# Windowed attention: how the reciprocals of the softmax sums reach the context's layout

## The chip, the core and the metric

The kernel runs on one core of a Trainium2 chip. The metric is the device time of one execution in microseconds, the median of three runs. A core has five engines that run side by side and meet at semaphores: TensorE (PE, matrix products and transposes into PSUM), VectorE (DVE), ScalarE (ACT), GpSimd (POOL) and SyncE (SP), which here only issues DMAs.

## What is computed

A chain of small layers over x of 8 sequences of 256 tokens with 128 features: a plain attention and a mixture of experts, a linear attention, a windowed transformer, a rotary attention, a second windowed transformer, a latent attention, and a last plain attention with experts. The change is in the two windowed transformers. Each has 6 layers; a layer has 16 heads of 64 and looks back over windows of 32 keys. Its attention, cut to what matters (dots mark what is left out):

```python
sim = jnp.einsum('bhwie,bhwje->bhwij', bq, bk2) * QK_SCALE
sim = jnp.where(mask, -jnp.finfo(sim.dtype).max, sim)
attn = jax.nn.softmax(sim, -1)
out = jnp.einsum('bhwij,bhwje->bhwie', attn, bv2)
...
return out @ Wo
```

The division by the sum of each softmax row is what the change is about: the kernel multiplies the context by the reciprocals afterwards.

## The kernel before

`windowed_transformers` goes through 48 **turns** per transformer, one for each layer and sequence (`TURNS = DEPTH * B`, turn T is layer T // 8, sequence T % 8). A turn has 8 **slots**, one for each pair of heads p. Every engine has its own hand-written order of work: `pe_window`, `act_window`, `dve_window` and the loop over `pool_spread` and `pool_prepare` go through the slots of turn T. In its slots they also prepare the queries, keys and values of turn T + 1 (`pe_chunks` L1784, the squares, copies and rotations at L2003, L2007, L2121, L2129, the turned queries and keys L1807, L2015, L2115) and do the output projection and feed-forward part of the turns before (`pe_out` L1819, `pe_gates` L1850, and others). An engine that waits holds back all that stands behind it in its order.

One pair goes this way. The 128 partitions hold the queries of one half (t = 0 or 1) of the 256 tokens.

- PE makes the scores (L1716); DVE adds the mask and takes the row minimum (L2090); ACT makes the exponentials and their row sums (`act_probs` L1983), into `pair_sums`, four columns per pair: two halves by two heads ("sides").
- DVE takes the four reciprocals in slot p (`dve_recip` L2099). They stand with queries on the partitions.
- PE turns the exponentials (L1728, L1729) in slot p, ACT copies them out of PSUM (L1990), and in slot p + 1 PE weighs the values with them (`pe_weigh` L1750). The context stands in PSUM bank 4 or 5, columns 0 to 255, with the 64 features of the two heads on the partitions and the 256 queries along the row.
- So the reciprocals have to be turned too, and repeated over 64 partitions. POOL spreads them to 128 x 256 (`pool_spread` L1944), PE transposes the two halves into the other half of the same bank (`pe_shares` L1738, slot p + 1), ACT copies them to `shares` (`act_copy_shares` L1995, at the end of slot p + 1), and DVE multiplies (`dve_share` L2104, slot p + 2, directly behind the reciprocal of that slot).

SP issues only the weights' loads, each as soon as its tile is free; they come at the start of each layer, so once in 8 turns, and are all in one sequence.

Of the kernel before, what the change touches and what calls it, by code (L numbers as in the profile page):

```python
# [16 lines left out]
P = 128  # L17
# [6 lines left out]
DH = 64  # L24
# [69 lines left out]
def allocate(nc, ctx):  # L94
# [36 lines left out]
    c.pair_sums = sb("pair_sums", [P, 4, HALVES, 2])  # L131
    c.shares = sb("shares", [P, 2, S])
    c.recip = sb("recip", [P, 2, 32])
    c.spread = sb("spread", [P, 2, S])
# [1475 lines left out]
WEIGHT_ORDER = (2, 0, 4, 3, 1, 5)  # L1610
PE_CHUNK_SLOTS = {j: (2 * j, 2 * j + 1) for j in range(6)}
# [15 lines left out]
def windowed_transformers(nc, sem, c, name, io):  # L1627
# [7 lines left out]
             "probs_ready", "probsT_in_psum", "probsT_ready", "prev_ready", "recip_ready", "spread_ready", "ctx_in_psum", "shares_ready", "ctx_ready",  # L1635
# [8 lines left out]
     s.probs_ready, s.probsT_in_psum, s.probsT_ready, s.prev_ready, s.recip_ready, s.spread_ready, s.ctx_in_psum, s.shares_ready, s.ctx_ready,  # L1644
     s.out_in_psum, s.shifted_in_psum, s.normed, s.normedT_in_psum, s.normedT_ready,
     s.gates_in_psum, s.linear_in_psum, s.gelu_ready, s.hidden_ready, s.ff_out_in_psum) = [sem(name + "_" + n) for n in names]
    wqkv_loaded = [sem(name + "_wqkv_loaded" + str(k)) for k in range(CHUNKS)]
    step = Count(steps)
    wqkv, wo = c.wA[:, :], c.wB[:, :]
    w1, w2 = c.wC[:, :], c.wD[:, :]  # L1650

# [44 lines left out]
    def run(number):  # L1696
        T0, T1 = number * TURNS, (number + 1) * TURNS

        def has_turn(turn):
            return T0 <= turn < T1  # L1700
# [31 lines left out]
        def pe_shares(pe, T, p):  # L1732
            pe.wait_ge(s.spread_ready, T * PAIRS + p + 1)
            if T * PAIRS + p - 1 > T0 * PAIRS:

                pe.wait_ge(s.ctx_ready, T * PAIRS + p - 1)
# [150 lines left out]
        def pe_window(pe, T):  # L1887
            following = has_turn(T + 1)
            for p in range(PAIRS):
                pe_turn_probs(pe, T, p)  # L1890
                if p >= 1:
                    pe_shares(pe, T, p - 1)
                elif has_turn(T - 1):
                    pe_shares(pe, T - 1, PAIRS - 1)
# [27 lines left out]
        def pe_tail(pe):  # L1922
            L = T1 - 1
            pe_shares(pe, L, PAIRS - 1)
# [13 lines left out]

        def pool_spread(g, T, p):
            g.wait_ge(s.recip_ready, T * PAIRS + p + 1)  # L1940
            if T * PAIRS + p - 2 >= T0 * PAIRS:

                g.wait_ge(s.ctx_in_psum, T * PAIRS + p - 1)
            g.tensor_copy(c.spread[:, p % 2, :].rearrange("p (n d) -> p n d", n=4),  # L1944
                          c.recip[:, 0, 4 * (p % 4):4 * (p % 4) + 4].unsqueeze(2).broadcast_to((P, 4, DH))
                          ).then_inc(s.spread_ready, 1)
# [31 lines left out]
        def act_probs(a, T, p, side):  # L1978
            if side == 0:
                a.wait_ge(s.negmax_ready, T * PAIRS + p + 1)  # L1980
            for t in range(HALVES):
                tile = c.pairs[:, 2 * (p % 4) + side, AT[t]:AT[t] + SPAN[t]]
                last = a.activation(tile, tile, ACT.Exp, scale=-1.0, bias=c.negmax[:, 2 * p + side, t:t + 1],  # L1983
                                    accum_out=c.pair_sums[:, p % 4, t, side:side + 1])
# [55 lines left out]
        def act_window(a, T):  # L2040
            following = has_turn(T + 1)
            for p in range(PAIRS):
# [19 lines left out]
                if p >= 1:  # L2062
                    act_copy_shares(a, T, p - 1)
                elif has_turn(T - 1):
                    act_copy_shares(a, T - 1, PAIRS - 1)
# [6 lines left out]
        def act_tail(a):  # L2072
            L = T1 - 1
            act_copy_shares(a, L, PAIRS - 1)
# [22 lines left out]
        def dve_recip(v, T, p):  # L2097
            v.wait_ge(s.probs_ready, T * PAIRS + p + 1)
            v.reciprocal(c.recip[:, 0, 4 * (p % 4):4 * (p % 4) + 4],  # L2099
                         c.pair_sums[:, p % 4, :, :].rearrange("p t h -> p (t h)")).then_inc(s.recip_ready, 1)  # L2100

        def dve_share(v, T, p):
            v.wait_ge(s.shares_ready, T * PAIRS + p + 1)
# [163 lines left out]

        with nc.Block() as block:

            @block.sync  # L2270
            def _(sp):
                sp.dma_start(c.rope[:, :, :, 0:DH], w["rope"]).then_inc(tables_loaded, 16)
                for d in range(layer_of(T0), layer_of(T1)):
                    T, first = d * B, d * B == T0

                    if not first:
                        sp.wait_ge(s.tables_ready, d)
                    sp.dma_start(c.scl[:, :, :].rearrange("p a b -> p (a b)"),
                                 w["scales"][d].partition_broadcast(P)).then_inc(s.scales_loaded, 16)
                    for k in WEIGHT_ORDER:  # L2280

                        if not first:
                            sp.wait_ge(s.chunk_in_psum, (T - 1) * N_CHUNKS + CHUNK_ORDER.index((1, k)) + 1)
                        sp.dma_start(wqkv[:, k * 512:(k + 1) * 512],
                                     w["wqkv"][d][:, k * 512:(k + 1) * 512]).then_inc(wqkv_loaded[k], 16)

                    if not first:
                        sp.wait_ge(s.out_in_psum, T)
                    sp.dma_start(wo, w["wo"][d]).then_inc(s.wo_loaded, 16)

                    if not first:
                        sp.wait_ge(s.linear_in_psum, T)
                    sp.dma_start(w1, w["w1"][d]).then_inc(s.ff_loaded, 16)

                    if not first:
                        sp.wait_ge(s.hidden_ready, T * 3)
# [228 lines left out]
```

## Time and profile before

| | us |
|---|---|
| median of 3 runs | 6057.9 (6055.31 to 6059.08) |
| the profiled execution's span | 6062.1 |
| PE, DVE, ACT, POOL busy in it | 5372.5, 4241.2, 3913.4, 2700.1 |
| head pairs in the two windowed transformers | 768 |

All durations come from one profiled execution with the span above. Matmuls are pipelined: the rows of successive ones overlap, and what one costs is the distance between their starts. A row with "x2" merges two instructions that follow each other. What stands in brackets is the idle time of the engine ahead of the row, and what ended it.

### The profile page before, as it was taken

How to read it: one execution, taken by the hardware profiler on the slowest of the kernel's cores; microseconds unless marked ns; L12 is line 12 of the kernel's file. 1: busy time of each engine (PE TensorE's matmuls, PEld its weight loads, DVE VectorE, ACT ScalarE, POOL GpSimd, SP SyncE). 2: the span in 40 equal slices, each digit the busy share in tenths (PEclk: the TensorE clock that was granted, in tenths of full speed). 3: DMA queues.
4: the chain of work that ended last, by engine and by line, in shares of the span. 5: the costliest groups of instructions: out<-in, count | busy, mean ns of one | idle time of the engine just before them, and what ended most of it. 6: DMA issues, size and time to landing. Idle time of an engine off the chain costs nothing. (4 is left out here: it accounts for less than half of the span.)

```text
span 6062.1 us, 121575 instructions
## 1 busy us (share of the span) xinstructions
PE 5372.5 (89%) x41154; PEld 3794.5 (63%) x41154; DVE 4241.2 (70%) x16112; ACT 3913.4 (65%) x11510; POOL 2700.1 (45%) x2578
## 2 busy tenths in 40 slices
PE   7885699999999999997489999999999999697989
PEld 5674366666666666665256666666666666464678
DVE  4453688888888888885378888788888887454522
ACT  2211588888888888884178888888888888222333
POOL 0000556556565565652166656566565665230000
PEclk9996799999999999998599999999999999697999
DMA  0000000000000000000000000000000000000000
GB/s 11 22 1 3 22 1 12 9 12 9 1 15 6 12 9 12 8 1 4 21 1 7 10 6 12 9 12 9 4 13 6 12 8 1 5 2 4 2 29 8
DMA packets 30964, 53.45 MB, mean 9 GB/s; under 512 B 7688, under 2 KB 17168, under 8 KB 29712
## 3 DMA queue, kind: packets, MB, share of 16 engines
q1 hardware_dynamic: 30352, 45.66, 2.4%
q8 instruction: 339, 5.55, 0.4%
q14 instruction: 273, 2.24, 0.1%
HBM read 44.60 MB, written 1.05 MB: 8 GB/s over the span
## 5 line engine op out<-in xcount | busy, mean ns | idle before, releaser
L1784 PE MATMUL bank<-wA,next_rowT 128*128 128x512 f32 x2304 | 1213.7, 629 | 194.6 <-DVE turnB L2129 73.1
L1983 ACT ACTIVATE pairs<-pairs,negmax 128x128 f32<-128x128 f32 (+1 forms) x3072 | 1236.8, 418 | 18.6 <-DVE negmax L2090 17.5
L1960 POOL TENSOR_TENSOR turnA<-raw,ropes 128x512 f32<-128x512 f32 x768 | 968.7, 1271 | 169.3 <-ACT raw L2007 140.4
L2090 DVE CUSTOM_DVE_ANT_0 pairs<-bank,bands,big 128x128 f32<-128x128 f32 (+1 forms) x3072 | 941.7, 364 | 64.6 <-PE bank L1716 61.0
L1967 POOL TENSOR_TENSOR qk<-turnA,turnB 128x512 f32<-128x512 f32 x768 | 975.8, 1271 | 0.0
L1944 POOL COPY spread<-recip 128x256 f32<-128x256 f32 x768 | 305.3, 398 | 1257.8 <-DVE recip L2099 1251.4
L1784 PEld LDWEIGHTS bank<-wA,next_rowT 128*128 128x128 f32 x2304 | 369.6, 190 | 676.7 <-DVE turnB L2129 294.3
L1990 ACT ACTIVATE pairsT<-bank 128x512 f32<-128x512 f32 x768 | 465.9, 607 | 302.2 <-PE bank L1729 301.9
L1983 ACT ACTIVATION_READ_ACCUMULATOR pairs<-pairs,negmax 128x1 f32 x3072 | 625.0, 203 | 0.0
L285 POOL TENSOR_TENSOR rstd<-vareps,neg_half 128x2 f32<-128x2 f32 x56 | 39.0, 696 | 1292.4 <-DVE vareps L256 892.7
L2129 DVE TENSOR_TENSOR turnB<-bank,ropes 128x512 f32<-128x512 f32 x768 | 523.1, 681 | 0.0
L1973 POOL TENSOR_TENSOR qk<-qk,big 128x1024 f32<-128x1024 f32 x192 | 365.7, 1905 | 341.3 <-DVE recip L2204 327.9
L1807 PE MATMUL bank<-ident,qk 128*128 128x128 f32 x3072 | 431.1, 279 | 41.5 <-ACT big L2010 16.4
L2007 ACT ACTIVATE raw<-bank 128x512 f32<-128x512 f32 x768 | 461.1, 600 | 0.0
L1807 PEld LDWEIGHTS bank<-ident,qk 128*128 128x128 f32 x3072 | 344.7, 142 | 156.1 <-issue 131.6
L1728 PE MATMUL bank<-ident,pairs 128*128 128x128 f32 x1536 | 383.4, 277 | 27.7 <-ACT pairs L1983 27.7
L1729 PE MATMUL bank<-ident,pairs 128*128 128x128 f32 x1536 | 377.7, 273 | 0.0
L1819 PEld LDWEIGHTS bank<-wB,ctxT 128*128 128x128 f32 x3072 | 357.8, 192 | 8.4 <-issue 0.3
L1819 PE MATMUL bank<-wB,ctxT 128*128 128x128 f32 x3072 | 358.8, 275 | 0.0
L1728 PEld LDWEIGHTS bank<-ident,pairs 128*128 128x128 f32 x1536 | 216.1, 141 | 178.3 <-ACT pairs L1983 90.8
L2104 DVE TENSOR_TENSOR ctxT<-bank,shares 128x256 f32<-128x256 f32 x768 | 306.1, 399 | 8.6
L1850 PE MATMUL bank<-xT,wC 128*128 128x256 f32 (+1 forms) x1152 | 305.4, 402 | 6.9 <-ACT big L2038 3.7
(306 smaller groups left out, 11272.8 us busy)
## 6 DMA issues: line engine op xcount, KB each, us to landing
wA<-in_wt_wqkv SPq DMA_DIRECT2D x72, 256.0 KB, 2.8
wB<-in_wt_wo SPq DMA_DIRECT2D x12, 512.0 KB, 3.5
wC<-in_wt_w SPq DMA_DIRECT2D x12, 341.0 KB, 2.9
wD<-in_wt_w SPq DMA_DIRECT2D x12, 192.0 KB, 2.4
big<-in_e_up SPq DMA_DIRECT2D x1, 2048.0 KB
big<-in_e_down SPq DMA_DIRECT2D x1, 2048.0 KB
scl<-in_wt_scales SPq DMA_DIRECT2D x12, 128.0 KB, 3.1
X<-in_x SPq DMA_DIRECT2D x8, 128.0 KB, 2.5
```

Of the source, the lines that this page charges most:

```text
L1728: pe.transpose(out[:, 0:P], probs[:, 0:P], c.ident[:, :])
L1729: last = pe.transpose(out[:, P:2 * P], probs[:, P + WINDOW:2 * P + WINDOW], c.ident[:, :])
L1784: pe.matmul(side_bank(i)[:, :], c.next_rowT[:, t * P:(t + 1) * P], wqkv[:, k * 512:(k + 1) * 512], start=True, stop=True).then_inc(s.chunk ...
L1807: done = pe.transpose(side_bank(i)[:, (2 * k + t) * P:(2 * k + t + 1) * P], c.qk[:, t, which, at:at + P], c.ident[:, :])
L1819: done = pe.matmul(c.bank[6][:, t * D:(t + 1) * D], ctxT[T % 2][:, k, t * P:(t + 1) * P], wo[:, k * D:(k + 1) * D], start=(k == 0), stop=( ...
L1960: g.tensor_tensor(c.turnA[:, m % 2, :].rearrange("p (h d) -> p h d", h=8), c.raw[:, m % 4, :].rearrange("p (h d) -> p h d", h=8), cos, ALU ...
L1967: g.tensor_tensor(c.qk[:, t, k // 2, (k % 2) * 512:(k % 2) * 512 + 512], c.turnA[:, m % 2, :], c.turnB[:, m % 4, :], ALU.add).then_inc(s.s ...
L1983: last = a.activation(tile, tile, ACT.Exp, scale=-1.0, bias=c.negmax[:, 2 * p + side, t:t + 1], accum_out=c.pair_sums[:, p % 4, t, side:si ...
L1990: a.activation(whole_blocks(c.pairsT[:, 2 * (p % 2):2 * (p % 2) + 2, :]), c.bank[2][:, :].rearrange("p (n k) -> p n k", n=4), ACT.Identity ...
L2007: last = a.activation(c.raw[:, m % 4, :], src, ACT.Identity)
L2090: last = v.tensor_tensor_reduce(c.pairs[:, 2 * (p % 4) + side, AT[t]:AT[t] + SPAN[t]], c.bank[side][:, AT[t]:AT[t] + SPAN[t]], c.bands[:, ...
L2129: v.tensor_tensor(out, turned, sin.unsqueeze(1).broadcast_to((P, 8, 2, DH // 2)), ALU.mult).then_inc(s.chunk_rotated, 1)
```

## The change

The spread copy, the two transposes and the copy of the shares are taken out, with their semaphores and the tile `spread`. In their place SP stores the four reciprocals of a pair, [128, 4], to a row of a small ring in DRAM so that each column becomes a line of 128 numbers (512 runs of 4 bytes), waits for it to land, and loads two lines that follow each other, 256 numbers, into each half of `shares`, repeated over 64 partitions. `pair_sums` changes the order of its columns to suit. `dve_share` waits for the context in PSUM and for the two loads. PE's wait for a free bank moves from `pe_shares` to `pe_weigh`. SP's program now goes slot by slot (`sp_window`): store, then the weights' loads that fall into this slot, then the two loads.

```diff
-        def pe_shares(pe, T, p):
-            pe.wait_ge(s.spread_ready, T * PAIRS + p + 1)
...
-            for t in range(HALVES):
-                pe.transpose(c.bank[4 + p % 2][:, S + t * P:S + (t + 1) * P], c.spread[:, p % 2, t * P:(t + 1) * P],
-                             c.ident[:, :])
         def pe_weigh(pe, T, p):
             pe.wait_ge(s.probsT_ready, T * PAIRS + p + 1)
             pe.wait_ge(s.prev_ready, T * PAIRS + p + 1)
+            if T * PAIRS + p - 1 > T0 * PAIRS:
+
+                pe.wait_ge(s.ctx_ready, T * PAIRS + p - 1)
...
-        def pool_spread(g, T, p):
...
-        def act_copy_shares(a, T, p):
-            a.wait_ge(s.ctx_in_psum, T * PAIRS + p + 1)
-            a.activation(c.shares[:, p % 2, :], c.bank[4 + p % 2][:, S:2 * S], ACT.Identity).then_inc(s.shares_ready, 1)
...
         def dve_share(v, T, p):
-            v.wait_ge(s.shares_ready, T * PAIRS + p + 1)
+            v.wait_ge(s.ctx_in_psum, T * PAIRS + p + 1)
+            v.wait_ge(s.shares_loaded[p % 2], 32 * (T * (PAIRS // 2) + p // 2 + 1))
             v.tensor_tensor(ctxT[T % 2][:, p, :], c.bank[4 + p % 2][:, 0:S], c.shares[:, p % 2, :],
                             ALU.mult).then_inc(s.ctx_ready, 1)
...
+        def sp_store_recip(sp, T, p):
+
+            sp.wait_ge(s.recip_ready, T * PAIRS + p + 1)
+            with nc.allow_non_contiguous_dma(reason="one column of reciprocals becomes one line"):
+                sp.dma_start(ring[p % 4].rearrange("n q -> q n"),
+                             c.recip[:, 0, 4 * (p % 4):4 * (p % 4) + 4]).then_inc(s.recip_stored, 16)
+
+        def sp_load_shares(sp, T, p):
+
+            sp.wait_ge(s.recip_stored, 16 * (T * PAIRS + p + 1))
+            if T * PAIRS + p - 1 > T0 * PAIRS:
+
+                sp.wait_ge(s.ctx_ready, T * PAIRS + p - 1)
+            for side in range(2):
+                sp.dma_start(c.shares[DH * side:DH * side + DH, p % 2, :],
+                             ring[p % 4, 2 * side:2 * side + 2, :].rearrange("t q -> (t q)").partition_broadcast(DH)
+                             ).then_inc(s.shares_loaded[p % 2], 16)
...
+        def sp_window(sp, T):
+            def layer_starts(turn):
+                return T0 < turn < T1 and starts_layer(turn)
+            for p in range(PAIRS):
+                sp_store_recip(sp, T, p)
+                if layer_starts(T + 2):
+                    if p == 0:
+                        sp_scales(sp, T + 2, False)
+                    for k in SP_WQKV_SLOTS.get(p, ()):
+                        sp_wqkv(sp, T + 2, k, False)
+                if layer_starts(T) and p == 7:
+                    sp_wo(sp, T, False)
+                if layer_starts(T - 2):
+                    if p == 0:
+                        sp_w1(sp, T - 2, False)
+                    if p == 1:
+                        sp_cols(sp, T - 2, False)
+                    if p == 3:
+                        sp_w2(sp, T - 2, False)
+                sp_load_shares(sp, T, p)
```

## Rows read from the trace of the kernel before

**Rows 1.** Page, section 1: engine, busy us, share of span, instructions.
```profile
span 6062.1 us, 121575 instructions
PE 5372.5 (89%) x41154; PEld 3794.5 (63%) x41154; DVE 4241.2 (70%) x16112; ACT 3913.4 (65%) x11510; POOL 2700.1 (45%) x2578
```

**Rows 2.** Windows: stretch, length, busy us per engine, clock, DMA share, GB/s.
```profile
1617.10:1642.10 25.00, 23.56 (x161) 14.89 (x160) 24.07 (x88) 22.06 (x71) 20.01 (x20) 1.00 0.00 1
1642.10:1652.50 10.40, 10.06 (x79) 8.46 (x79) 6.00 (x34) 6.85 (x18) 5.91 (x5) 1.00 0.01 2
```

**Rows 3.** Timeline of PE, slots 6 and 0: start us, us, instruction, idle before.
```profile
1644.83 0.27 PE L1729 MATMUL bank<-ident,pairs 128*128 128x128 f32 x1
1644.94 0.38 PE L1738 MATMUL bank<-ident,spread 128*128 128x128 f32 x2
...
1646.62 1.99 PE L1850 MATMUL bank<-xT,wC 128*128 128x256 f32 x8
...
1656.32 0.33 PE L1728 MATMUL bank<-ident,pairs 128*128 128x128 f32 x1 [0.21 <-ACT pairs L1983]
```

**Rows 4.** Timeline of ACT, slots 6, 7 and 0.
```profile
1645.63 0.56 ACT L2029 ACTIVATE xT<-bank,cols 128x256 f32<-128x256 f32 x1
...
1656.08 0.19 ACT L1983 ACTIVATION_READ_ACCUMULATOR pairs<-pairs,negmax 128x1 f32 x1
...
1661.61 0.36 ACT L1995 ACTIVATE shares<-bank 128x256 f32<-128x256 f32 x1
1661.87 0.58 ACT L2003 ACTIVATE sq<-bank 128x512 f32<-128x512 f32 x1
```

**Rows 5.** Timeline of DVE: reciprocals and multiplications of one turn.
```profile
1612.90 0.17 DVE L2099 RECIPROCAL recip<-pair_sums 128x4 f32<-128x4 f32 x1
...
1617.10 0.18 DVE L2099 RECIPROCAL recip<-pair_sums 128x4 f32<-128x4 f32 x1 [1.08 <-ACT pairs L1983]
1617.37 0.42 DVE L2104 TENSOR_TENSOR ctxT<-bank,shares 128x256 f32<-128x256 f32 x1
...
1622.05 0.40 DVE L2104 TENSOR_TENSOR ctxT<-bank,shares 128x256 f32<-128x256 f32 x1
...
1631.10 0.17 DVE L2099 RECIPROCAL recip<-pair_sums 128x4 f32<-128x4 f32 x1
1631.19 0.39 DVE L2104 TENSOR_TENSOR ctxT<-bank,shares 128x256 f32<-128x256 f32 x1
...
1633.64 0.18 DVE L2099 RECIPROCAL recip<-pair_sums 128x4 f32<-128x4 f32 x1
...
1638.69 0.40 DVE L2104 TENSOR_TENSOR ctxT<-bank,shares 128x256 f32<-128x256 f32 x1
```

**Rows 6.** Page, section 5: busy us, mean ns of one, idle before.
```profile
L1944 POOL COPY spread<-recip 128x256 f32<-128x256 f32 x768 | 305.3, 398 | 1257.8 <-DVE recip L2099 1251.4
```

**Rows 7.** DMA issues: KB each, median us from issue to landing.
```profile
wA<-in_wt_wqkv SPq DMA_DIRECT2D x72, 256.0 KB, 2.8
...
scl<-in_wt_scales SPq DMA_DIRECT2D x12, 128.0 KB, 3.1
...
out<-X SPq DMA_DIRECT2D x8, 128.0 KB, 2.0
...
rope<-in_window_rope SPq DMA_DIRECT2D x2, 256.0 KB, 3.1
...
cols<-in_wt_cols SPq DMA_DIRECT2D x12, 4.0 KB, 1.6
...
rows<-in_a_bo SPq DMA_DIRECT2D x2, 64.0 KB, 3.6
```

**Rows 8.** Timeline of SP: the second column is the issue.
```profile
1130.53 0.43 SPq L2278 DMA_DIRECT2D scl<-in_wt_scales  x1
```

**Rows 9.** Timeline of DVE, end of the first transformer.
```profile
2803.11 0.17 DVE L2099 RECIPROCAL recip<-pair_sums 128x4 f32<-128x4 f32 x1
...
2805.92 0.92 DVE L2104 TENSOR_TENSOR ctxT<-bank,shares 128x256 f32<-128x256 f32 x2
```

More of the change, by code:

```diff
@@ L1610 @@
 WEIGHT_ORDER = (2, 0, 4, 3, 1, 5)
+SP_WQKV_SLOTS = {2: (2, 0), 3: (4,), 5: (3, 1), 6: (5,)}
 PE_CHUNK_SLOTS = {j: (2 * j, 2 * j + 1) for j in range(6)}
@@ L1647, in windowed_transformers @@
     wqkv_loaded = [sem(name + "_wqkv_loaded" + str(k)) for k in range(CHUNKS)]
+    s.shares_loaded = [sem(name + "_shares_loaded" + str(n)) for n in range(2)]
     step = Count(steps)
@@ new lines, in sp_scales, with sp_wqkv @@
+        def sp_scales(sp, T, first):
+            if not first:
+                sp.wait_ge(s.tables_ready, layer_of(T))
+            sp.dma_start(c.scl[:, :, :].rearrange("p a b -> p (a b)"),
+                         w["scales"][layer_of(T)].partition_broadcast(P)).then_inc(s.scales_loaded, 16)
+        def sp_wqkv(sp, T, k, first):
+            if not first:
+                sp.wait_ge(s.chunk_in_psum, (T - 1) * N_CHUNKS + CHUNK_ORDER.index((1, k)) + 1)
+            sp.dma_start(wqkv[:, k * 512:(k + 1) * 512],
+                         w["wqkv"][layer_of(T)][:, k * 512:(k + 1) * 512]).then_inc(wqkv_loaded[k], 16)
@@ new lines, in sp_wo, with sp_w1, sp_cols @@
+        def sp_wo(sp, T, first):
+            if not first:
+                sp.wait_ge(s.out_in_psum, T)
+            sp.dma_start(wo, w["wo"][layer_of(T)]).then_inc(s.wo_loaded, 16)
+        def sp_w1(sp, T, first):
+            if not first:
+                sp.wait_ge(s.linear_in_psum, T)
+            sp.dma_start(w1, w["w1"][layer_of(T)]).then_inc(s.ff_loaded, 16)
+        def sp_cols(sp, T, first):
+            if not first:
+                sp.wait_ge(s.hidden_ready, T * 3)
+            sp.dma_start(c.cols[:, 0:8], w["cols"][layer_of(T)]).then_inc(s.ff_loaded, 16)
@@ new lines, in sp_w2 @@
+        def sp_w2(sp, T, first):
+            if not first:
+                sp.wait_ge(s.ff_out_in_psum, T)
+            sp.dma_start(w2, w["w2"][layer_of(T)]).then_inc(s.w2_loaded, 16)
+        def sp_window(sp, T):
[18 more added lines that the diff above has]
+                sp_load_shares(sp, T, p)
@@ L2272, in _ @@
                 sp.dma_start(c.rope[:, :, :, 0:DH], w["rope"]).then_inc(tables_loaded, 16)
[L2273 to L2296, printed above, removed]
-                    sp.dma_start(c.cols[:, 0:8], w["cols"][d]).then_inc(s.ff_loaded, 16)
-                    if not first:
-                        sp.wait_ge(s.ff_out_in_psum, T)
-                    sp.dma_start(w2, w["w2"][d]).then_inc(s.w2_loaded, 16)
+                sp_scales(sp, T0, True)
+                for k in WEIGHT_ORDER:
+                    sp_wqkv(sp, T0, k, True)
+                sp_wo(sp, T0, True)
+                sp_w1(sp, T0, True)
+                sp_cols(sp, T0, True)
+                sp_w2(sp, T0, True)
+                for T in range(T0, T1):
+                    sp_window(sp, T)
                 sp.wait_ge(tables_loaded, 16 * (number + 1))
```

38 lines of the change are left out of this document (10 added, 28 removed).

## Prediction

> **What bounds the kernel now.** I read the page first [rows 1]: TensorE (PE) is busy 89% of the span, VectorE (DVE) 70%, ScalarE (ACT) 65%, GpSimd (POOL) 45%. These are means over stages with different limits. The change lies in the two windowed transformers, with 768 head pairs [rows 6]. Their rows repeat turn by turn, so one turn of 44.6 us (there are 96) is what has to be read. I then looked at one turn, from 1612.9 us on, in stretches [rows 2]. In one of 25.0 us DVE is busy 24.07 us: DVE alone sets the time. In the 10.4 us behind it PE is busy 10.06 us and DVE only 6.00. The 9.2 us that are left are filled by no engine: work is handed from PE to ACT to PE to DVE, and DVE waits 1.08 us a turn for ACT's exponentials [rows 5]. POOL waits 1251 us for DVE's reciprocals [rows 6]; it is ahead of the others.
>
> In order of time the chain of one turn is: PE turns the probabilities of pair 6, then the shares (1644.94), the scores, the weighing, the feed-forward gates (1646.62), the output projection and the probabilities of pair 7 [rows 3]; ACT copies those, loads a table, makes exponentials up to 1656.27 [rows 4]; PE starts on them at 1656.32 after a wait [rows 3] and does shares, scores, weighing and turned queries; ACT makes the exponentials of pair 1 of the next turn and copies the shares at 1661.61 [rows 4]; DVE, idle 1.08 us, takes the reciprocal and then multiplies by the shares (1617.10 and 1617.37 in the turn before, [rows 5]), and from there to 1642.1 it has no gap worth naming [rows 2].
>
> **What the change removes.** Per pair:
> - PE, two transposes of the spread reciprocals. Successive transposes start 0.11 us apart (1644.83 and 1644.94, and the two of one row last 0.38 us where one alone lasts 0.27), so the two hold PE for 0.22 us [rows 3]. All eight slots of a turn have them, but only two are on the chain, those of slots 6 and 0. In slots 1 to 5 DVE is the limit, and in slot 7 PE waits for the exponentials afterwards. Behind slot 6 the next that could be late is the normalised row for the gates: ACT ends it at 1646.19 [rows 4], the gates start at 1646.62, so 0.43 us of cover against 0.22 gained. Behind slot 0 ACT's copies wait for what PE makes there, so they move along. Gain 2 x 0.22 = 0.44 us a turn.
> - ACT, the copy of the shares: 0.36 us, but the next instruction starts 0.26 us behind it [rows 4]. It counts once a turn: DVE starts the multiplication 0.27 us after the reciprocal at 1617.10, where elsewhere it is 0.09 us (1631.10, 1631.19) [rows 5]. Gain 0.18 us a turn. The squares that DVE reduces next move up with it.
> - POOL, the spread copy, 0.4 us x768 [rows 6]: nothing, no engine was late for want of it.
>
> Sum 0.62 us a turn. In each transformer 47 turns follow another: 94 x 0.62 = 58.3 us.
>
> **What it adds.** Per pair one store and two loads, issued by SyncE (SP), and one more wait of DVE ahead of the multiplication. This second wait is for the context in PSUM, which is over a slot old by then. The trace has no such pair of waits at this place; its price is between 0 and the 0.09 us in which DVE starts one short instruction behind another [rows 5]. I take 0, because DVE's sequencer can take it while the engine is still at work, and keep 5 slots x 0.09 = 0.45 us a turn for the range.
>
> The real question is whether the shares are there when DVE asks. Behind a late multiplication stand, on DVE, the slot's transpose, reductions, rotations and minima, and PE and ACT wait for those. The time to spare runs from the end of reciprocal p to the start of multiplication p, two slots later [rows 5]. It is 7.42 us for pair 3 (1631.27 to 1638.69), the tightest. Pair 0 is next with 8.98 (1613.07 to 1622.05), pair 1 has 13.9 (1617.28 to 1631.19). What must fit into it:
> - the store, 512 separate runs of 4 bytes. The trace has no store of such runs. The nearest is the output store, 256 runs of 512 bytes, 2.0 us to landing. 256 KB in 1024 runs (the rope table) land in 3.1 us where 256 KB in 128 runs (wqkv) land in 2.8, so more runs cost little: 2.2 us. The upper end is the latest landing of any small DMA, 3.6 us. The lower one is the 1.6 us of 4 KB [rows 7].
> - the issue of the first load, 0.43 us, as for the scales' broadcast [rows 8].
> - the second load. It writes one 1 KB row to 64 partitions; the scales' broadcast writes such a row to 128 partitions and lands in 3.1 us, which I take; upper end 3.6 [rows 7].
> - three hand-overs by semaphore at 0.05 us (ACT ends at 1656.27, PE starts at 1656.32, [rows 3, 4]).
>
> Sum 2.2 + 0.43 + 3.1 + 0.15 = 5.9 us; upper end 3.6 + 0.43 + 3.6 + 0.15 = 7.8 us. Against 7.42 the first leaves 1.5 us of cover and costs nothing; the second delays pair 3 by 0.4 us a turn.
>
> SP works in order. It waits for each store and then issues two loads: 2.2 + 0.9 = 3.1 us a pair, against 2.54 us between reciprocals 3 and 4 [rows 5]. Store 4 goes out 0.6 us late and its way has two more slots of time: hidden. The weight loads now stand between a pair's store and its loads. They come in few turns (five layer starts a transformer); what each waits for was done in the slot before or earlier, and its issue falls into SP's wait for the store. What is left is its transfer ahead of the loads, about 1.2 us for 256 KB (2.8 against 1.6 for 4 KB, [rows 7]), most of it beside the store. With 1.5 us of cover: nothing.
>
> At the end of each transformer there is no cover. Reciprocal 7 of the last turn ends at 2803.28, and its multiplication, the second of a row, starts near 2806.4, 3.1 us later [rows 9]. A way of 5.9 us makes that 2.8 us later, twice: 6 us.
>
> **A rule against the change.** The Trainium skill, page "DMA: Bandwidth & Descriptors", section "Rules for kernel authors", says that a strided last dimension becomes one descriptor per element and is better rearranged; its section "Specifications" adds that below 512 B a transfer is a read-modify-write. The rope row shows many runs to be cheap at 256 B each; no row here shows 4-byte runs into HBM, so the rule stands as rival 1. The same page ("Anatomy of one DMA") puts the fixed cost of a DMA near 2.0 us; by that figure, an estimate, the two hops with the issue are about 4.5 us and the cover only grows.
>
> **Rivals.**
> 1. The store is slow (slower). Each of 16 DMA engines gets 32 of the 4-byte runs. If one costs 0.1 us and not almost nothing, the store takes 1.6 + 3.2 = 4.8 us and the way 8.5 us. DVE then stands 1.1 us at pair 3 inside its own stretch: 94 x 1.1 = 103 us, and 11 us at the two ends, against 58 gained: 6057.9 - 58 + 103 + 11 = 6114. The change loses from a way of 8.0 us on (7.42 + 0.62). For it: nothing shows such runs, and the cover is only 1.5 us. Against: the rope row. From 9.3 us on pair 0 stands too and it becomes 6200 and more.
> 2. The gain is mostly taken back (no change): pair 3 stands 0.4 us (the upper end above), or one of the three gains alone survives. Then 0.2 us a turn x 94 = 20, less 9 at the ends: 6047.
> 3. More than the chain is freed: PE's 0.22 us counts in every slot, 768 x 0.22 = 169 us, less 6: 5895; half way from there to the forecast, 5950. Against: DVE is busy 24.07 of 25.0 us [rows 2].
>
> That the change doesn't do what it says is no case here: the three operations are gone.
>
> **How the numbers follow.** The profiled span is 6062.1 us [rows 1], 4.2 over the median of the runs, 6057.9. Forecast 6062.1 - 58.3 + 6 = 6009.8 in the profile, 6006 as a median. Chances: forecast 0.57 (its own range 5985 to 6035, the added wait included), rival 1 0.21, rival 2 0.13, rival 3 0.09. The range reaches into half of rival 3 and takes in rival 1 as priced, without its worse part: 5970 to 6130. A measurement of this kernel can tell about 0.2% (12 us) from no change. Faster takes the forecast and rival 3, 0.66; same is 0.13; slower 0.21.
>
> **What would show it.** Right: turns of 44.0 us; 0.09 and not 0.27 us from reciprocal to multiplication in slot 1; the DVE stretch of 25.0 us as long as before, with no idle time put down to a DMA; stores landing near 2.2 us, loads near 3. Wrong: DVE idle ahead of the multiplication for the shares' load, in slot 5 first; SP waiting over 4 us for a store; or DVE's stretch longer without a wait, which would be the added wait itself. The prediction rests most on the 4-byte store, for which I have only rows of other forms.

## The result and the profile after

The changed kernel takes 9916.5 us (median of 4 runs, 9913.3 to 9926.2) where the kernel before took 6058.5 beside it: a ratio of 1.637 (95% interval 1.635 to 1.640). The forecast was 6006, its range 5970 to 6130. The span of its profiled execution is 9912.9 us.

The page of the kernel after, sections 1 and 2. The busy rows answer to [rows 1]; PEclk is TensorE's granted clock in 40 slices.

```profile
span 9912.9 us, 119371 instructions
...
PE 6344.5 (64%) x39618; PEld 4198.9 (42%) x39618; DVE 4200.0 (42%) x16112; ACT 3764.4 (38%) x10742; POOL 2427.4 (24%) x1810
...
PEclk9967777777777778777577777777777777776899
```

No engine is busier than before except PE (with its weight loads), whose granted clock is lower over most of the span (0.7 and 0.8 of full speed, where it was 1.00 in [rows 2]). Its costliest group, 629 ns a matmul before, shows the longer matmuls and the wait (busy us, mean ns, idle before):

```profile
L1780 PE MATMUL bank<-wA,next_rowT 128*128 128x512 f32 x2304 | 1845.3, 929 | 2511.1 <-DVE turnB L2103 1836.6
```

The time has gone into waits. The waits of SP (us in total, times, longest), then of DVE:

```profile
SPq L2256 <- DMA wt_ring<-recip: 6447.8, 764, 10.4
...
SPq L2246 <- DVE recip L2072: 94.1, 43, 36.8
```

```profile
DVE ctxT L2078 <- DMA shares<-wt_ring: 4132.9, 719, 14.1
```

The first row divides to 6447.8 / 764 = 8.4 us in which SP stands, per pair, until its store has landed. (At this place SP also waits for a free half of `shares`, but 764 of 768 waits are put down to the store.) The second says that SP almost never waits for a reciprocal: when its turn comes, the reciprocal is long there. So SP, not DVE, sets the pace, and DVE's 4133 us are the same time seen from the other side. TensorE's lower clock is not the cause: SP's round holds next to no wait for computed work. The timelines of SP and of DVE show the order (start us, duration, instruction; in brackets the idle time before it):

```profile
2006.44 1.08 SPq L2256 DMA_DIRECT2D shares<-wt_ring  x2
2007.57 0.59 SPq L2246 DMA_DIRECT2D wt_ring<-recip  x1
2017.48 1.08 SPq L2256 DMA_DIRECT2D shares<-wt_ring  x2
2018.61 0.58 SPq L2246 DMA_DIRECT2D wt_ring<-recip  x1
```

```profile
2002.45 0.42 DVE L2078 TENSOR_TENSOR ctxT<-bank,shares 128x256 f32<-128x256 f32 x1 [7.35 <-DMA shares<-wt_ring]
2010.87 0.17 DVE L2072 RECIPROCAL recip<-pair_sums 128x4 f32<-128x4 f32 x1
2016.00 0.42 DVE L2078 TENSOR_TENSOR ctxT<-bank,shares 128x256 f32<-128x256 f32 x1 [4.96 <-DMA shares<-wt_ring]
```

SP issues a store at 2007.57, and its loads only at 2017.48; the next store follows 0.05 us behind them. It was never two stores at a time. Over a transformer the stores follow each other every 10.5 us on the mean (8.4 of waiting, 0.6 and 1.1 of issues, the rest weights' issues); x 8 = 84 us. The mean turn, from one reciprocal 0 to the next over both transformers, is 84.15 us where it was 44.45 (the first turns are shorter than the 44.6 of the others): 94 x (84.15 - 44.45) = 3732 us of the 3851 by which the span grew.

The DMA issues, with the median time to landing, answer to [rows 7]:

```profile
shares<-wt_ring SPq DMA_DIRECT2D x1536, 64.0 KB, 3.6
wA<-in_wt_wqkv SPq DMA_DIRECT2D x72, 256.0 KB, 9.0
```

The loads land in 3.6 us, near the forecast 3.1. The weights, issued just ahead of them and behind the store, land after 9.0 us where it was 2.8. With the quick stores of `spaced64` and `runs16` below, in the same order of issue, it is 3.7 and 4.7, so most of the delay comes from the slow store and a part from the other DMAs.

### The profile page after: what moved, and what is told of

Its sections match the earlier page's. It is cut to its first block and busy times, and to the rows that moved or that the text cites. A ratio compares the mean times of both kernels' runs of the same rounds, so it can differ in the third digit from the quotient of the medians.

```text
span 9912.9 us, 119371 instructions
## 1 busy us (share of the span) xinstructions
PE 6344.5 (64%) x39618; PEld 4198.9 (42%) x39618; DVE 4200.0 (42%) x16112; ACT 3764.4 (38%) x10742; POOL 2427.4 (24%) x1810
## 5 line engine op out<-in xcount | busy, mean ns | idle before, releaser
L1780 PE MATMUL bank<-wA,next_rowT 128*128 128x512 f32 x2304 | 1845.3, 929 | 2511.1 <-DVE turnB L2103 1836.6
L1780 PEld LDWEIGHTS bank<-wA,next_rowT 128*128 128x128 f32 x2304 | 529.0, 264 | 3180.9 <-DVE turnB L2103 2089.1
L2063 DVE CUSTOM_DVE_ANT_0 pairs<-bank,bands,big 128x128 f32<-128x128 f32 (+1 forms) x3072 | 940.8, 363 | 19.4 <-PE bank L1718 13.2
L1981 ACT ACTIVATE big<-bank 128x512 f32<-128x512 f32 x384 | 229.4, 597 | 1559.2 <-PE bank L1780 1558.5
L1803 PE MATMUL bank<-ident,qk 128*128 128x128 f32 x3072 | 525.5, 320 | 441.4 <-DVE hT L2150 415.6
L1803 PEld LDWEIGHTS bank<-ident,qk 128*128 128x128 f32 x3072 | 412.5, 165 | 637.0 <-issue 589.0
L1981 ACT ACTIVATE sq<-bank 128x512 f32<-128x512 f32 x384 | 227.5, 593 | 754.3 <-PE bank L1780 754.1
L1730 PE MATMUL bank<-ident,pairs 128*128 128x128 f32 x1536 | 505.0, 343 | 8.5 <-ACT pairs L1965 8.5
L1731 PE MATMUL bank<-ident,pairs 128*128 128x128 f32 x1536 | 499.0, 340 | 0.0
L1718 PE MATMUL bank<-big 64*128 64x128 f32 (+1 forms) x3072 | 368.9, 369 | 80.8 <-DVE negmax L2063 58.6
L1718 PE MATMUL bank<-kT,qT 64*128 64x128 f32 (+1 forms) x3072 | 367.5, 368 | 49.2 <-DVE negmax L2063 31.5
L1731 PEld LDWEIGHTS bank<-ident,pairs 128*128 128x128 f32 x1536 | 281.8, 183 | 242.0 <-issue 241.9
```

The costliest lines, as they stand in the source:

```text
L1718: last = pe.matmul(c.bank[side][:, AT[t]:AT[t] + SPAN[t]], q[:, t * P:(t + 1) * P], k[:, FIRST_KEY[t]:FIRST_KEY[t] + SPAN[t]], start=True, ...
L1730: pe.transpose(out[:, 0:P], probs[:, 0:P], c.ident[:, :])
L1731: last = pe.transpose(out[:, P:2 * P], probs[:, P + WINDOW:2 * P + WINDOW], c.ident[:, :])
L1780: pe.matmul(side_bank(i)[:, :], c.next_rowT[:, t * P:(t + 1) * P], wqkv[:, k * 512:(k + 1) * 512], start=True, stop=True).then_inc(s.chunk ...
L1803: done = pe.transpose(side_bank(i)[:, (2 * k + t) * P:(2 * k + t + 1) * P], c.qk[:, t, which, at:at + P], c.ident[:, :])
L1981: a.activation(sq[m % 4], src, ACT.Square).then_inc(s.chunk_squared, 1)
```

## The experiments

An **interval** p below (the expectations say slot p) is the time from reciprocal p to the next one on DVE, the median over the first transformer's turns from the second on, worked out from the starts of the rows that [rows 5] samples. The last column is the median turn. The ratio is to runs of the kernel before made beside each.

| run | median us | ratio (95%) | intervals 0 to 7, us | turn |
|---|---|---|---|---|
| before | 6059 to 6061 | 1 | 4.20 4.86 9.14 2.54 4.97 6.48 7.46 4.98 | 44.6 |
| removed | 6113.4 | 1.009 (1.008 to 1.011) | 4.20 4.66 10.15 2.54 4.96 6.49 7.46 4.76 | 45.2 |
| runs16 | 6115.1 | 1.009 (1.008 to 1.011) | 4.20 4.68 10.13 2.56 4.96 6.49 7.46 4.76 | 45.2 |
| spaced64 | 6120.4 | 1.010 (1.008 to 1.012) | 4.20 4.68 10.13 2.56 4.97 6.49 7.46 4.76 | 45.3 |
| moved | 6033.5 | 0.996 (0.995 to 0.997) | 4.14 4.66 9.14 2.54 4.96 6.48 7.46 4.98 | 44.4 |
| removed_gated | 6019.0 | 0.993 (0.992 to 0.995) | 4.20 4.66 9.18 2.54 4.97 6.48 7.46 4.76 | 44.3 |
| runs16_gated | 6022.7 | 0.994 (0.992 to 0.996) | 4.20 4.68 9.15 2.56 4.97 6.49 7.46 4.76 | 44.3 |
| add_later | 5971.5 | 0.985 (0.984 to 0.987) | 4.20 4.86 8.06 2.63 4.96 6.49 7.46 4.98 | 43.7 |
| moved3 | 5960.8 | 0.984 (0.982 to 0.985) | 4.12 4.66 8.15 2.74 4.97 6.49 7.46 4.98 | 43.6 |
| two_in_flight | 7781.2 | 1.284 (1.281 to 1.286) | 6.49 7.95 9.84 2.56 11.34 7.12 7.46 5.40 | 61.6 |
| row | 7867.5 | 1.298 (1.296 to 1.301) | 6.36 9.87 11.23 2.56 9.79 9.46 7.46 5.46 | 62.9 |
| row_gated_later | 7864.3 | 1.298 (1.296 to 1.300) | 6.35 9.86 11.23 2.56 9.78 9.68 7.46 5.46 | 63.0 |

### Is it the store, or the hops? (runs16)

The store is laid out as 128 runs of 16 bytes; loads, waits and SP's order stay.

```diff
-                sp.dma_start(ring[p % 4].rearrange("n q -> q n"),
+                sp.dma_start(ring[p % 4].rearrange("n q -> (n q)").rearrange("(q n) -> q n", n=4),
```

> The changed kernel with its store as 128 runs of 16 bytes and not 512 of 4; the loads are as they were, so the shares come in another order (this changes the result). If the landing of the store is all that went wrong and follows the count of runs, it lands in 2 + 128 x 0.014 = 3.8 us, SP's loop is 3.8 + 1.8 = 5.6 us a pair, about the 5.5 us of a slot, and the kernel takes 6000 to 6200 us. If the two loads or DVE's added wait were at fault, it stays above 7000 us.

Measured: 6115.1 us. The waits of SP and DVE in this run, to be laid beside those of the kernel after:

```profile
SPq L2246 <- DVE recip L2072: 1955.9, 638, 36.8
...
SPq L2256 <- DMA wt_ring<-recip: 1073.0, 759, 3.3
```

```profile
DVE ctxT L2078 <- DMA shares<-wt_ring: 4.0, 3, 1.8
```

SP now stands 1073.0 / 759 = 1.4 us for a store and has time to wait for reciprocals; DVE waits 4 us in all. The way through DRAM is hidden. 3800 us hang on how the store is cut into runs.

### What makes a 4-byte store slow? (probes, probes2, spaced64, probes3)

To the kernel before, one DMA was added on SP in every second slot, on data nobody uses; the kind changes every four turns, so each is measured 32 times. SP's loads of weights go slot by slot in these runs, and SP waits for each added DMA.

```diff
+            kind, dst = (T % TURNS) // 4, probed
...
+                sp.dma_start(*pair).then_inc(s.probed, 16)
```

> The kernel before, with one more DMA on SP for every second pair that nobody but SP waits for, of another kind every four turns: 512 runs of 4 bytes to DRAM next to each other, 64 bytes apart, 4 KB apart; 128 runs of 16 bytes; 256 and 128 runs of 4 bytes; 128 runs of 128 bytes; 128 runs of 4 bytes into one SBUF partition; 512 runs of 4 bytes read from DRAM; 128 runs of 512 bytes; 128 runs of 16 bytes SBUF to SBUF. Theory A (each short write into DRAM costs, about 14 ns in a single file, wherever it goes): 512 runs 9 us at every spacing, 256 runs 5.5, 128 runs 3.7 with 4 or 16 or 128 bytes, and near 2 us for SBUF and for the read. Theory B (short writes that share a line of DRAM stand behind each other): 9 us next to each other, near 2.5 us at 4 KB spacing. Theory C (the engines are slow with many short runs, wherever they go): the read of 512 runs takes 9 us too. The kernel's time stays at 6058 within 0.5%.

> The kernel before, with one unrelated DMA on SyncE in every second slot; twelve kinds, eight turns of four DMAs each, 32 apiece; what is read is the time from issue to landing. In the first such run 128, 256 and 512 runs of 4 bytes that fill whole lines of DRAM landed after 7.3 to 8.3 us, 512 runs 64 bytes apart after 1.8. Theory B (4-byte runs into one and the same stretch of DRAM stand behind each other): the landing depends on how many runs share a stretch. 512 runs 8 bytes apart would land after 4 to 6 us, 16 bytes apart 3 to 4, 32 bytes apart about 2.5; one stretch of 64 bytes in 16 runs would be as late as 512 runs, about 7; 8 runs about 4, 4 runs about 3, 2 runs about 2. 1024 runs 64 bytes apart: 2.2. 128 runs of 8 bytes that follow each other: 3 to 4; of 32 bytes: 1.4. Theory A (each small run costs, whatever its neighbour): 1024 spaced runs would be far later than 512 spaced ones, and 2 or 4 runs would be at 1.4. The time of the kernel itself stays within 0.2% of before.

> The kernel before with unrelated DMAs again, 32 of each kind. The second such run left the theory that 4-byte runs into one stretch of 64 bytes stand behind each other short: 16 runs that fill a single stretch landed after 1.3 us, 128 that fill eight after 7.3. New: 32, 64 and 128 runs that fill 2, 4 and 8 stretches; 128 runs that fill the same eight stretches in two other orders (neighbouring partitions 32 and 64 bytes apart); 16 partitions of four columns (64 runs, 4 stretches); 128 runs 8, 16 and 64 bytes apart; four columns to places 4 KB apart. Theory S (each of the 16 DMA engines takes neighbouring partitions one after the other, and its next write waits for its last one into the same 64 bytes): 16 to 64 partitions grow from 1.3 by the writes an engine has in a stretch, 128 runs with neighbours 64 bytes apart land at 1.4 to 2. Theory E (writes of different engines into one stretch hold each other up, and it takes several in turn): the other orders are no faster, or slower. Theory C (count of runs in the DMA): the 64-byte spacing is as late as the dense one.

The three runs, one execution each, take 6060.9, 6063.7 and 6106.7 us; in the last, the first transformer has turns of 46.6 to 53.2 us where the kind that lands after 13.2 us is issued: the weights behind it on SP come late (in one such turn ACT stands 3.25 us for `cols`). Microseconds from issue to the last landing, median, out of the trace's semaphore updates ("dense": neighbouring values 4 bytes apart in DRAM):

| stores to DRAM | us | | us |
|---|---|---|---|
| 512 x 4 B, dense | 8.3 to 9.2 | 16 x 4 B, dense (one 64 B stretch) | 1.3 |
| 512 x 4 B, 8 B apart | 3.5 | 32 x 4 B, dense (2) | 3.1 |
| 512 x 4 B, 16 B apart | 2.6 | 64 x 4 B, dense (4) | 6.7 |
| 512 x 4 B, 32 B apart | 2.0 | 128 x 4 B, dense (8) | 7.2 |
| 512 x 4 B, 64 B apart | 1.8 | the same 8, neighbours 32 B apart | 8.0 |
| 512 x 4 B, 4 KB apart | 1.8 | the same 8, neighbours 64 B apart | 6.7 |
| 1024 x 4 B, 64 B apart | 2.6 | 16 partitions x 4 columns, dense (4) | 6.3 |
| 128 x 8 B, dense | 2.9 | 128 x 4 B, 8 / 16 / 64 B apart | 3.0 / 1.4 / 1.4 |
| 128 x 16 B, dense | 1.4 | 4 dense columns in 4 pages | 13.2 |

| others | us |
|---|---|
| 128 x 4 B into one SBUF partition | 1.9 |
| 512 x 4 B read from DRAM into SBUF | 2.1 |
| 2, 4, 8 x 4 B into DRAM, dense | 1.0, 1.1, 1.1 |
| 256 x 4 B into DRAM, dense | 7.8 |
| 128 x 32 B, 128 B, 512 B into DRAM | 1.4, 1.4, 1.5 |

The count of runs is not it: 512 spaced runs land as fast as 128 x 128 B (1.4) but for 0.4 us, 64 dense ones take 6.7. Nor is it the form of the descriptors: the same 4-byte runs are quick into SBUF, or out of DRAM. It is the packing of 4-byte *writes into DRAM*: at one, two, four, eight and sixteen values per 64 bytes 512 runs take 1.8, 2.0, 2.6, 3.5 and 8.3. The order of partitions hardly matters (7.2, 8.0, 6.7), which is against the theory that each DMA engine holds up its own next write. But a single filled stretch of 64 bytes was expected at 7 and lands at 1.3, half and a quarter of one were expected at 4 and 3 and land at 1.1, and it takes four filled stretches to reach the plateau. Shown is that the packing does it, from two to four filled stretches on. That writes of several DMA engines into one stretch hold each other up would fit; the mechanism itself stays open, and so does why four pages are worse than one.

The Trainium skill, page "DMA: Bandwidth & Descriptors", section "Specifications", says that below 512 B a transfer is a read-modify-write. A time to landing can't show whether one takes place; if it does, it is not what makes a store this late: dense runs of 16 bytes, far below 512 B, land in 1.4 us, as do runs of 128 B, and runs of 512 B in 1.5. Its section "Rules for kernel authors" puts a transposition by a rearranged pattern 19 times behind the hardware's own. No run here uses the hardware's own; against the same 512 numbers stored without a transposition the pattern costs 8.3 to 1.4 us, 6 times.

Then the same in the changed kernel: each value gets 64 bytes of the ring. The loads read the row of the scales, so the context is multiplied by those.

```diff
-                sp.dma_start(ring[p % 4].rearrange("n q -> q n"),
+                sp.dma_start(ring[p % 4].rearrange("n (q z) -> q n z", z=16)[:, :, 0],
```

> The changed kernel with each of the 512 values stored into a stretch of 64 bytes of its own in DRAM; the number of 4-byte runs stays 512. The two loads read 256 numbers of a row of the weights' scales in place of the ring, so the context is multiplied by those and not by the reciprocals. Theory B (what is slow is several 4-byte writes into the same 64 bytes): store lands at 1.8 us, all of it is hidden, 6113 us as with the three operations removed. Theory A (512 runs of 4 bytes are slow as such): stays at 9900.

Measured: 6120.4 us. The store, still 512 runs of 4 bytes:

```profile
wt_ring<-recip SPq DMA_DIRECT2D x768, 2.0 KB, 2.0
```

It lands in 2.0 us, near the 2.2 that the forecast had taken. Of the store only the packing in DRAM was changed; the loads read another row of the same size.

### Is SP's order the bound? (two_in_flight)

SP issues store p before it waits for store p - 1 and issues that pair's loads. Nothing else changes.

> The changed kernel, but SyncE issues the store of pair p before it waits for the store of pair p - 1 and issues that pair's loads: two stores may be under way at once. Theory L (the bound is SyncE's loop of store, landing, two loads, at 10.56 us a pair, and a landing is a latency that two stores share): a pair takes at least 10.56 / 2 = 5.3 us, little under the 5.6 of a pair in the kernel before, and with the longer way to VectorE some slots still wait: 6300 to 7200 us. Theory W (the 4-byte writes are a throughput limit: the second store stands behind the first): a pair takes at least the 8.4 us of a landing, 67 us a turn, 6115 + 94 x (67 - 45) = 8200 us or more, and the landings grow. Rival (only VectorE's wait for one pair's way counts, not SyncE's loop): no gain or a loss, since every pair's way gets longer, at or over 9916.

Measured: 7781.2 us, between the two theories' ranges.

```profile
SPq L2247 <- DVE recip L2073: 3264.0, 719, 37.2
...
SPq L2257 <- DMA wt_ring<-recip: 1066.6, 423, 7.3
```

```profile
DVE ctxT L2079 <- DMA shares<-wt_ring: 2012.4, 553, 13.6
```

SP has stopped being the bound: it waits 3264 us for reciprocals. A landing is a latency that two stores share: out of the semaphore updates, where one store is issued less than 3.5 us behind another (74 times), both land after 8.5 us in the median, as the others do (9.2 in the kernel after). The second does not stand behind the first. So the in-order loop was worth at least 9917 - 7781 = 2135 us of the loss. What is left is the pair's own way, longer than the time to its multiplication, and longer than in the kernel after by one thing: a pair's loads now stand behind the next pair's reciprocal. DVE waits 2012 us, in intervals 0, 1 and 4 above all.

### Where did the forecast gain go? (removed, moved, removed_gated)

`removed` takes the three operations out and puts nothing in their place: no ring, no DMA; the context is multiplied by a constant, so the division by the softmax sums is left out.

> The three operations are gone and nothing is put in their place: no store, no loads, DVE multiplies by a constant that stands in shares (this leaves the division by the softmax sums out). Theory 1 (the chain of one turn as read from the trace of before, 0.62 us a turn): 94 x 0.62 = 58 us less, about 6000 us, the turn 44.0 us. Rival (PE's 0.22 us counts in every slot): 169 us less, 5890 us. Rival (only one of the three gains survives): 6035 us.

Measured: 6113.4 us, 0.9% **slower** than before, with less work on three engines. The table says where: intervals 1 and 7 are 0.20 and 0.22 us shorter, interval 2 is 1.01 us longer. 94 x (1.01 - 0.42) = 55 us, and 54 were measured. Here are GpSimd and DVE at the end of interval 2 of the kernel before (reciprocal 3 is at 1631.10):

```profile
1627.04 1.27 POOL L1967 TENSOR_TENSOR qk<-turnA,turnB 128x512 f32<-128x512 f32 x1
1631.34 0.40 POOL L1944 COPY spread<-recip 128x256 f32<-128x256 f32 x1 [3.02 <-DVE recip L2099]
1631.69 1.26 POOL L1967 TENSOR_TENSOR qk<-turnA,turnB 128x512 f32<-128x512 f32 x1
```

```profile
1627.10 1.24 DVE L2166 TENSOR_SCALAR big<-big 128x2 f32<-128x2 f32 x1
1628.37 0.18 DVE L2145 TENSOR_SCALAR big<-big 128x34 f32<-128x34 f32 x1
```

and in `removed`:

```profile
1638.11 2.50 POOL L1947 TENSOR_TENSOR qk<-turnA,turnB 128x512 f32<-128x512 f32 x2
```

```profile
1638.17 1.23 DVE L2137 TENSOR_SCALAR big<-big 128x2 f32<-128x2 f32 x1
1639.44 1.22 DVE L2116 TENSOR_SCALAR big<-big 128x34 f32<-128x34 f32 x1
```

A VectorE step on two numbers per partition lasts 1.24 us and ends at 1628.34, 0.03 us behind GpSimd's addition (1627.04 + 1.27). Its neighbour, on 34 numbers, takes 0.18. In the kernel before one step is caught like this. The spread copy then makes GpSimd wait 3.02 us for the reciprocal, and the next addition (1631.69) falls behind DVE's steps for the square roots. Without the copy two additions stand back to back, and catch two steps. The first step ends at 1639.40, the second at 1640.66, 0.05 us behind the additions. The copy that I had priced at nothing was a gate. The Trainium skill, page "SBUF — State Buffer", section "Who interferes with whom", calls the port pair that the two engines share an exclusive lock; the ends of these rows agree with that.

`removed_gated` is that kernel with the wait put back, without the copy:

```diff
                     for p in range(PAIRS):
+                        g.wait_ge(s.recip_ready, T * PAIRS + p + 1)
                         pool_prepare(g, T + 1, p)
```

> The run without ring, spread, transposes and copy (multiplication by a constant, so the division by the softmax sums is left out), and GpSimd waits in each slot for VectorE's reciprocals where its spread copy had waited. Theory G (the copy's wait had kept GpSimd's next addition off VectorE's square roots, whose last step otherwise stands 1.05 us behind it): slot 2 is back at 9.14 us, the turn is 44.2, the 0.42 us of slots 1 and 7 come through: 6059 - 94 x 0.42 = 6019 us. Rival (slot 2 is longer for another reason, the lower load on TensorE or its clock among them): stays at 6113.

Measured: 6019.0 us; interval 2 is 9.18, and step L2116 is back at 183 ns from 1213 (DVE's groups, busy us and mean ns; `removed` first, `removed_gated` second):

```profile
L2116 DVE TENSOR_SCALAR big<-big 128x34 f32<-128x34 f32 x90 | 109.1, 1213 | 3.1
```

```profile
L2116 DVE TENSOR_SCALAR big<-big 128x34 f32<-128x34 f32 x90 | 16.5, 183 | 3.1
```

`moved` leaves everything in and only takes TensorE's share transposes of pairs 5 and 7, and ScalarE's copy of pair 7, out of the places where I had counted them.

```diff
-                if p >= 1:
+                if p >= 1 and p != 6:
                     pe_shares(pe, T, p - 1)
...
+                if p == 7:
+                    pe_shares(pe, T, 7)
```

> The kernel before with nothing taken out: PE's transposes of the shares of pair 5 stand before the turned queries of slot 5 and those of pair 7 at the end of slot 7, where PE waits for ACT anyway, and ACT copies the shares of pair 7 before the turned queries of slot 0, where it is idle 0.40 us. If the chain of one turn was read rightly, this takes the same 0.4 to 0.62 us a turn off it as the removal: 38 to 58 us less, 6000 to 6020 us. If the gain needs the operations gone, it stays at 6058.

Measured: 6033.5 us, 26 us gained where 38 to 58 were forecast. Interval 1 gains its 0.20 us (ScalarE's copy), interval 0 only 0.06, and interval 6, whose transposes are gone, nothing. The rows suggest why. First PE and DVE of the kernel before, then of `removed`, in slot 6:

```profile
1645.28 0.77 PE L1716 MATMUL bank<-kT,qT 64*128 64x128 f32 x8
```

```profile
1644.48 0.69 DVE L2115 COPY kT<-bank 128x512 f32<-128x512 f32 x1 [1.48 <-PE bank L1807]
1645.09 0.17 DVE L2099 RECIPROCAL recip<-pair_sums 128x4 f32<-128x4 f32 x1
```

```profile
1657.37 0.77 PE L1716 MATMUL bank<-kT,qT 64*128 64x128 f32 x8 [0.17 <-issue]
```

```profile
1656.58 0.69 DVE L2086 COPY kT<-bank 128x512 f32<-128x512 f32 x1 [1.48 <-PE bank L1801]
1657.19 0.17 DVE L2070 RECIPROCAL recip<-pair_sums 128x4 f32<-128x4 f32 x1
```

The scores start 0.19 and 0.18 us behind the start of the reciprocal, with the transposes ahead of them or without. They need the keys that DVE copies (L2115, in `removed` L2086) just ahead of that reciprocal, and start 0.11 and 0.10 us behind the end of that copy; without the transposes PE idles 0.17 us. In slot 7 it is the other way round. DVE's copy waits for TensorE there (the kernel before, then `removed`):

```profile
1656.14 0.69 DVE L2115 COPY kT<-bank 128x512 f32<-128x512 f32 x1 [1.17 <-PE bank L1807]
```

```profile
1668.02 0.69 DVE L2086 COPY kT<-bank 128x512 f32<-128x512 f32 x1 [0.96 <-PE bank L1801]
```

TensorE has the transposes of pair 6 ahead of that in slot 7, so `removed` gains 0.22 us in interval 7 (the idle time falls from 1.17 to 0.96). The transposes in slot 0 lie on a path beside it, from ScalarE's exponentials to the scores. That both must get shorter, and together give 0.22 us once, fits `moved`, which had left those of pair 6 in place: 0.06. No run takes those of pair 6 away alone, so this part is argued and not shown.

### The two causes taken away at once (runs16_gated)

The store of `runs16` and the wait of `removed_gated` in the changed kernel; the multiplication uses reciprocals of other queries.

> The changed kernel with the store as 128 runs of 16 bytes (each value still lands in the ring, in another order, so the context is multiplied by the reciprocals of other queries) and with GpSimd waiting for VectorE's reciprocals in each slot. Each half was measured alone: this store without the wait 6115, the wait without any DMA 6019. If the store, the two loads and VectorE's wait for them cost nothing once the 4-byte writes are gone: 6019 again. If the DMAs lie on the path where GpSimd no longer holds slot 2 back: 6030 or more.

Measured: 6022.7 us, 3.7 over the run without any DMA, whose own executions lie 12 us apart. With both causes gone the change is worth 0.6% (0.994, 0.992 to 0.996). The store, the two loads and the added wait cost next to nothing.

### A ring in SBUF (row, row_gated_later)

Since 4-byte writes into SBUF are quick, a complete version keeps the ring there: four stores, one for each column, into one partition's row.

```diff
+                for n in range(4):
+                    sp.dma_start(c.row[p % 4:p % 4 + 1, P * n:P * n + P].unsqueeze(2),
+                                 c.recip[:, 0, 4 * (p % 4) + n:4 * (p % 4) + n + 1]).then_inc(s.recip_stored, 16)
```

> The changed kernel with the ring in SBUF: four DMAs write the four columns of reciprocals, 128 runs of 4 bytes each, into one partition's row, and the two loads repeat it over 64 partitions. Everything is computed. In the first probes 128 runs of 4 bytes into one SBUF partition landed after 1.9 us. If only the 4-byte writes into DRAM were slow, the way is hidden: 6113 us as with the three operations removed (GpSimd's addition still beside VectorE's roots). Rival (five more DMAs a pair fill SyncE's order, or SBUF's partition is the bottleneck of the repeated reads): a way over 7.4 us shows first in slot 5, and 6150 to 6600 us.

> The same, with the wait for the reciprocals kept on GpSimd and its last addition of slot 2 in slot 3. The pieces measured apart: 5971.5 with the addition later, and 0.42 us a turn for the removed steps on the path (6059 to 6019 with the wait kept): 5971.5 - 40 = 5932 us, faster than both kernels. Rival (as above): 5970 or more.

Measured: 7867.5 and 7864.3 us. My expectation failed. The rival's cause held, SP's order fills up, but not its 6150 to 6600 us.

```profile
2014.60 4.00 SPq L2247 DMA_DIRECT2D row<-recip  x4
2021.25 1.16 SPq L2257 DMA_DIRECT2D shares<-row  x2
2022.45 4.00 SPq L2247 DMA_DIRECT2D row<-recip  x4
```

```profile
shares<-row SPq DMA_DIRECT2D x1536, 64.0 KB, 5.3
```

Four stores issued in 4.00 us, 1905.3 / 768 = 2.5 us of waiting for them, two loads in 1.16: 7.85 us from one pair to the next (2014.60 to 2022.45), x 8 = 62.8 us, and 62.9 is its turn. The same arithmetic as for the changed kernel, with another store. The loads, which all read one partition, land after 5.3 us where `runs16` had 2.7; that is on each pair's way and not in the loop. The wait on GpSimd and the later addition, 1.5% each where DVE sets the time, bring nothing (7867.5, 7864.3): the loop is full, and in `row` no step is caught anyway (its step on two numbers, L2140, takes 170 ns).

### The caught step of the kernel before (add_later, moved3)

The kernel before pays for one caught step a turn itself. `add_later` moves one of GpSimd's additions behind the spread copy of the next slot; `moved3` adds the moves of `moved`, and puts ScalarE's copy of the next queries ahead of the share copy in slot 7.

```diff
-POOL_SLOTS = {1: ("cos0", "cos1", "add0"), 2: ("cos2", "add1", "cos3", "add2"), 3: ("add3", "scale0"),
+POOL_SLOTS = {1: ("cos0", "cos1", "add0"), 2: ("cos2", "add1", "cos3"), 3: ("add2", "add3", "scale0"),
```

> The kernel before; only GpSimd's last addition of slot 2 stands in slot 3. Theory G: in the kernel before one small VectorE step of the roots (L2166) lasts 1.24 us beside a GpSimd addition, where its twin takes 0.18. If the addition comes later, none does: 94 x 1.06 = 100 us less, 5959 us, if what stands behind (the sums to TensorE's transposes in slot 3) is not late. Rival (the addition is itself on the path to the turned keys, or falls on other VectorE steps): 6040 to 6110 us.

> The kernel before with TensorE's share transposes of pairs 5 and 7 and ScalarE's copy of pair 7 moved off the chain (these alone measured 6033.5), ScalarE's copy of the next turn's first queries ahead of the share copy in slot 7, and GpSimd's addition in slot 3. Gains add up if they lie in different slots: 0.26 + 0.12 to 0.2 us a turn for the first and 1.06 for the addition: 6059 - 94 x 1.5 = 5918 us. Rival: the addition brings nothing: 6020.

`add_later` takes 5971.5 us, 1.5% less than before (5959 was forecast); L2166 has fallen from 1157 ns to 172:

```profile
L2166 DVE TENSOR_SCALAR big<-big 128x2 f32<-128x2 f32 x96 | 16.5, 172 | 3.3
```

Interval 2 gains 1.08 us, interval 3 loses 0.09. `moved3` was to give 5918 and gave 5960.8: intervals 0 and 1 gain 0.28 us, but 2 and 3 lose 0.20 of it against `add_later`. The cause stays open. It is the fastest version here, without the change under study.

## Why the prediction was wrong, point by point

- **The 4-byte store** (2.2 us, upper end 3.6): about 9 us, 8.4 of waiting and 0.6 of issue. The step that failed is the choice of the nearest row: runs of 256 and 512 bytes bound a count of runs, and the count was not what costs. `spaced64` measured the term as forecast, 2.0 us, for the same count. Rival 1 named the right suspect with the wrong law, 0.1 us for each run of an engine: 1024 spaced runs land in 2.6 us, 32 dense ones in 3.1.
- **What a late store costs.** Even with the store at its measured 9.2 us the forecast's formula was short: it makes the way 9.2 + 0.43 + 3.1 + 0.15 = 12.9 us, so that pairs 3 and 0, the two it held to be tight, would stand 5.5 and 3.9 us, an estimate of about 6006 + 94 x 9.4 = 6900 us. Rival 1 priced a delay of DVE at single pairs ("6200 and more") and let the pairs overlap. SP's loop was worked out, 3.1 us a pair, but compared only with the 2.54 us between two reciprocals, and not repeated for the rival's 4.8. The rule that was missing: a queue that waits in order has a period, 8.4 + 0.6 + 1.1 us and the weights' issues, to be held against the 5.6 us of a pair, and it does not hide behind anything once it is over. `two_in_flight` shows this, `row` shows it again.
- **The gain, 0.62 us a turn**: 0.42. ScalarE's copy gave 0.20 where 0.18 was forecast. Of TensorE's twice 0.22 only one arrived, and by the rows that one needed the transposes in slot 7, which I had ruled out. The 0.43 us of cover that I named in slot 6 was for the gates; the operand that was late there was the keys' copy on DVE.
- **GpSimd's copy, "nothing"**: it cost 94 x 1.0 us to lose it, more than the whole gain. The page's 1251 us of waiting for reciprocals [rows 6] was read as slack. It was also the order between two engines that disturb each other. This is a cost of the quick versions (`removed`, `runs16`, `spaced64`) and no part of the 9916.5 - 6058.5 = 3858 us: in the changed kernel SP's loop has moved GpSimd's additions off those steps, and they take 206 and 228 ns (busy us, mean ns, idle before):

```profile
L2140 DVE TENSOR_SCALAR big<-big 128x2 f32<-128x2 f32 x96 | 19.8, 206 | 3.3
L2119 DVE TENSOR_SCALAR big<-big 128x34 f32<-128x34 f32 x90 | 20.5, 228 | 3.1
```

- **The added wait, 0**: right. `runs16_gated` lies within 4 us of `removed_gated`.
- **The loads, 3.1 us**: 3.6 beside the slow store, 2.7 in `runs16`. **The way hidden**: right once the store is quick, DVE waits 4 us in all.
- **The signs.** Two of those named as wrong came: SP waits over 4 us for a store, and DVE is idle ahead of the multiplication for the loads, though not in slot 5 above all but at 719 of 768 pairs.
- **The fixed cost of 2.0 us** that the prediction took from the Trainium skill is given, in the section it names, for DMAs that GpSimd issues. SP issues these, and the quick small stores landed after 1.0 to 2.6 us. The forecast's sum did not use it.

## What to carry to other kernels

Before a DMA hop is put on an in-order queue, add up one round of that queue, waits for landings included, and hold it against the time of one unit of work: if it is longer, the queue is the kernel. Scatter small values into DRAM with neighbours 16 bytes apart or more, or in runs of 16 bytes, not as many packed 4-byte writes (512 numbers: 2.6 us at 16 bytes, 1.8 at 64, 8.3 packed). When an operation is removed, ask what its wait kept apart: a long GpSimd operation may fall on a short VectorE step, and a two-element step that lasts over 1 us in the trace marks the place.

## What the hardware showed unexpectedly

- Packed 4-byte writes into DRAM: 16 of them land after 1.3 us, 64 after 6.7, 512 after 8.3 to 9.2, and 512 with 64 bytes each after 1.8. With such a store ahead of them, 256 KB of weights land after 9.0 us, with a quick one ahead after 3.7 to 4.7, in the kernel before after 2.8. Two such stores at once take no longer than one (8.5 us).
- A VectorE TENSOR_SCALAR of 128x2 lasts 1.24 us beside a GpSimd addition and 0.17 without.
- The issue of a one-column store to one SBUF partition holds SP for 0.47 us alone, and 1.0 us each when four follow each other.
